# C products of a state-space stage on GpSimd, fed by DMA and summed in PSUM

## The reference

```
u = silu(conv1d(u) + conv1d_b);  x_dbl = u @ x_proj_w.T
dt, Bm, Cm = x_dbl[..., :8], x_dbl[..., 8:16], x_dbl[..., 16:]
delta = softplus(dt @ dt_proj_w.T + dt_proj_b);  A = -exp(A_log)
# for every position t:
h = exp(delta_t * A) * h + (delta_t * u_t) * B_t      # (D, N)
y_t = sum over n of h[:, n] * C_t[n]
# then
y = (y + u * D_param) * silu(z);  out = y @ out_proj_w.T
```

## Time and profile before

| | us |
|---|---|
| median of 3 runs (450.05 to 451.16) | 450.65 |
| the profiled execution | 448.37 |
| its span | 446.7 |
| busy TensorE / VectorE / ScalarE / GpSimd | 366.8 / 330.4 / 302.2 / 177.2 |
| first scan starts / last scan starts | 153.13 / 302.46 |

### The profile page before, as it was taken

The page is one execution under the profiler, slowest core; times in us unless marked ns, Lnnn a source line. Parts: engine busy times, 40 slices in busy tenths (PEclk is TensorE's granted clock), DMA queues, the critical chain, the costliest instruction groups (busy, mean ns, idle before and its releaser), DMA issues. The chain is left out here.

```text
span 446.7 us, 10932 instructions
## 1 busy us (share of the span) xinstructions
PE 366.8 (82%) x4013; PEld 240.8 (54%) x4013; DVE 330.4 (74%) x603; ACT 302.2 (68%) x619; POOL 177.2 (40%) x149
## 2 busy tenths in 40 slices
PE   5699999999995959986785746567797989999996
PEld 5567777777653421432242212123484649888885
DVE  1779887787832896799987999996666876655554
ACT  2389899999855897588759925518985454454543
POOL 7134223313103339839955996766171220000000
PEclk9679999999998995689987966868999999999999
DMA  6110000005040320050000000000030000111111
GB/s 157 6 20 6 1 0 1 0 0 119 9 106 20 72 54 1 2 124 0 0 0 1 1 0 0 0 0 1 1 74 1 1 2 15 19 24 21 21 21 26
DMA packets 24447, 10.34 MB, mean 23 GB/s; under 512 B 20976, under 2 KB 22768, under 8 KB 24416
## 3 DMA queue, kind: packets, MB, share of 16 engines
q1 hardware_dynamic: 23624, 9.87, 10.8%
q10 hardware_dynamic: 792, 0.07, 0.2%
HBM read 2.00 MB, written 1.61 MB: 8 GB/s over the span
## 5 line engine op out<-in xcount | busy, mean ns | idle before, releaser
L1357 PE MATMUL pair<-BCf,sel 96*128 96x392 bf16 x128 | 38.2, 392 | 32.8 <-DVE Hs L1947 28.8
L493 POOL TENSOR_TENSOR YA<-YA,hC 128x784 f32<-128x784 f32 x27 | 51.0, 1887 | 31.1 <-DVE hC L1963 30.1
L1947 DVE TENSOR_TENSOR_SCAN Hs<-dA,pair 128x784 f32<-128x784 f32 x32 | 57.1, 1785 | 1.2 <-ACT dA L833 0.3
L462 POOL TENSOR_TENSOR Km<-Ks,mask 128x784 f32<-128x784 f32 x16 | 24.1, 1507 | 69.2 <-ACT Ks L713 69.2
L1357 PEld LDWEIGHTS pair<-BCf,sel 96*128 96x128 bf16 x128 | 10.2, 104 | 71.2 <-issue 68.5
L1836 DVE TENSOR_REDUCE mx<-pair 128x8 f32<-128x392 f32 x64 | 33.0, 556 | 19.2 <-PE pair L1145 19.2
L1940 DVE TENSOR_TENSOR pair<-DU,pair 128x784 f32<-128x784 f32 x32 | 31.1, 973 | 11.1 <-PE pair L1357 10.7
L1183 PE MATMUL pair<-ident,Pr 128*128 128x128 f32 x256 | 38.5, 284 | 0.5 <-ACT Pr L700 0.5
L1656 PE MATMUL pair<-hst,BD 128*128 128x112 f32 x224 | 37.0, 295 | 2.2 <-DVE Rt L2242 0.5
L1183 PEld LDWEIGHTS pair<-ident,Pr 128*128 128x128 f32 x256 | 29.0, 144 | 11.5 <-issue 9.6
L1656 PEld LDWEIGHTS pair<-hst,BD 128*128 128x128 f32 x224 | 29.2, 190 | 9.5 <-DVE hst L2236 5.4
(11 more groups left out here) (259 smaller groups left out, 885.6 us busy)
## 6 DMA issues: line engine op xcount, KB each, us to landing
SX<-XP SPq DMA_DIRECT2D x48, 112.2 KB
XT<-in_x SPq DMA_DIRECT2D x4, 392.0 KB, 6.3
out<-Os SPq DMA_DIRECT2D x28, 56.0 KB, 1.7
AD<-Aa SPq DMA_DIRECT2D x4, 196.0 KB
NB<-in_L_conv_x_proj_w SPq DMA_DIRECT2D x4, 3.0 KB
DW<-in_L_conv_dw SPq DMA_DIRECT2D x4, 1.1 KB
W<-in_L_conv_w_qkv ACTq DMA_DIRECT2D x1, 48.0 KB
vec<-in_L_conv_b_qkv ACTq DMA_DIRECT2D x3, 0.5 KB
```

The source lines that it names most:

```text
L493: eng.tensor_tensor(y, y, hC[:, n % NHC, :], ALU.add).then_inc(g_ya, 1)
L1357: ins = eng.matmul(SPREAD[s][:, columns(h)], sel[:, n, :], upper(BCf[:, c % 2, s, columns(h)]), start=True, stop=True)
L1947: eng.tensor_tensor_scan(Hs[:, n % 2, :], dA[:, n % NA, :], SPREAD[0], 0.0, ALU.mult, ALU.add).then_inc(v_s, 1)
```

## The change

C no longer goes through TensorE's spread. B and C are projected in one product of 128 columns: rows 0 to 95 hold three copies of B for the bf16 parts, rows 96 to 127 the 8 rows of C of the four groups. A DMA on SP's queue hands row n of C to all channels, in one of four buffers Cs. GpSimd multiplies the states by it (`times_c`), with four buffers of states and three of products, and TensorE adds the products into PSUM (STATES, pair 1) with 32 x 32 pieces of the identity (`total`). VectorE loses its C products; its B product comes in halves of 392 columns, each of which waits for its half of the spread alone. The softplus drops the correction's factor exp(-log(u)) = 1/u, takes the log from another table set, and writes the relu straight into DL; for image 0 VectorE does relu and the copy of the projection. The orders of all engines are written anew.

```diff
-        PAIR = dict(B=0, C=1, conv=2, u=2, delta=2, xC=2, xB=3, wout=3, out=3, var=3, z=3, x2=3)
+        PAIR = dict(B=0, conv=2, u=2, delta=2, xB=2, wout=3, out=3, var=3, z=3, x2=3)
...
+            def c_rows(c, *states):
+                for n in states:
+                    i = DS * c + n
+                    if n == 0:
+                        eng.wait_ge(c_["xB"], c + 1)
+                    if i >= NCS:
+                        eng.wait_ge(v_c, i - NCS + 1)
+                    eng.dma_start(Cs[i % NCS][:, :], bcast(BCf[3 * C + n:P:DS, c % 2, :], 1, C)).then_inc(s_cs[i % NCS], 16)
+            shifted_copies(0)
+            shifted_copies(1)
+            c_rows(0, 0, 1, 2, 3)
+            shifted_copies(2)
+            c_rows(0, 4, 5, 6, 7)
+            c_rows(1, 0, 1)
+            shifted_copies(3, (0,))
+            c_rows(1, 2)
+            shifted_copies(3, (1,))
+            c_rows(1, 3)
+            shifted_copies(3, (2,))
+            c_rows(1, 4, 5, 6, 7)
+            c_rows(2, *range(DS))
+            c_rows(3, *range(DS))
...
+            def times_c(c, *states):                       # GpSimd
+                for n in states:
+                    i = DS * c + n
+                    eng.wait_ge(s_cs[i % NCS], 16 * (i // NCS + 1))
+                    eng.wait_ge(v_s, i + 1)
+                    if i >= NHC:
+                        eng.wait_ge(y_s, i - NHC + 1)
+                    eng.tensor_tensor(hC[:, i % NHC, :], Hs[:, i % NHS, :], Cs[i % NCS][:, :], ALU.mult).then_inc(v_c, 1)
...
                 elif i == 1:                               # GpSimd, pool_ssm
+                    times_c(1, 0, 1)
                     remainder(2)
+                    times_c(1, 2)
+                    split(2)
+                    times_c(1, 3, 4)
                     plus_log(2)
                     delta(2)
+                    times_c(1, 5)
                     scaled(0)
+                    times_c(1, 6, 7)
...
                 elif i == 1:                               # ScalarE, act_ssm
                     silu_u(2, 0)
                     silu_u(2, 1)
                     silu_z(1)
+                    exponents()                            # a table load
                     decays(1, 4)
                     sp_abs(2, 0)
                     sp_abs(2, 1)
                     sp_e(2)
                     sp_u(2)
                     sp_u1(2)
                     decays(1, 5)
                     sp_relu(2)
                     copy_bc(2)
                     out_m(0)
                     decays(1, 6)
                     var_ln(0)
                     var_exp(0)
                     decays(1, 7)
+                    log(2)                                 # a table load and sp_l
                     silu_conv(3, 0)
                     silu_conv(3, 1)
                     silu_x2(2)
+                    exponents()
                     decays(2, 0, 1, 2, 3)
...
+            def add_up(src, h, first=False, last=False):   # TensorE
+                for g in range(G):
+                    rows = slice(C * g, C * g + C)
+                    ins = eng.matmul(STATES[rows, h, :], ident[rows, rows], src[rows, columns(h)], start=first, stop=last)
+                return ins
...
+                elif i == 1:                               # TensorE, pe_ssm
+                    spread(1, 1)
+                    total(0, 6, 7)
+                    inner(2, 1)
+                    spread(1, 2)
+                    total(1, 0)
+                    gate(1)
+                    delta(2, 0)
+                    delta(2, 1)
+                    spread(1, 3)
+                    total(1, 1)
+                    x_b(2)
+                    spread(1, 4)
+                    total(1, 2)
+                    out(0)
+                    spread(1, 5)
+                    total(1, 3)
+                    conv(3, 0)
+                    var(0)
+                    spread(1, 6)
+                    total(1, 4)
+                    conv(3, 1)
+                    spread(1, 7)
+                    total(1, 5)
+                    x2(2)
+                    spread(2, 0)
+                    total(1, 6)
+                    inner(3, 0)
...
             def times_b(c, n):                             # VectorE
                 eng.wait_ge(v_du, c + 1)
+                for h in range(2):
+                    eng.wait_ge(p_["B"], 2 * (DS * c + n) + h + 1)
+                    eng.tensor_tensor(SPREAD[:, columns(h)], DU[:, c % 2, columns(h)], SPREAD[:, columns(h)], ALU.mult).then_inc(v_b, 1)
             def scan(c, n):
+                i = DS * c + n
+                eng.wait_ge(v_b, 2 * i + 2)
+                eng.wait_ge(a_da, i + 1)
+                if i >= NHS:
+                    eng.wait_ge(v_c, i - NHS + 1)
+                eng.tensor_tensor_scan(Hs[:, i % NHS, :], dA[:, n % NA, :], SPREAD, 0.0, ALU.mult, ALU.add).then_inc(v_s, 1)
...
+            def first_rows():                              # VectorE, image 0, inside the last attention step
+                eng.wait_ge(p_["xB"], 1)
+                eng.tensor_copy(halves(BCf[:, 0, :]), result("xB", 0)).then_inc(c_["xB"], 1)
+                remainder(0)
```

More of the change, by code:

```diff
@@ L560, in pool_ssm @@
                 if i == 0:
-                    add(0, 1)
-                    split(1, 0, "xB")
-                    remainder(1)
-                    add(0, 2)
+                    times_c(0, 0, 1, 2, 3, 4)
+                    split(1)
                     plus_log(1)
-                    add(0, 3)
                     delta(1)
-                    split(1, 1, "xC")
-                    add(0, 4)
-                    add(0, 5)
-                    add(0, 6)
-                    add(0, 7)
+                    times_c(0, 5, 6, 7)
@@ L954, in act_ssm @@
                     decays(2, 7)
-                    decays(3, 0, 1, 2, 3)
+                    log(3)
                     silu_z(3)
                     silu_x2(3)
+                    exponents()
+                    decays(3, 0, 1, 2, 3)
                 else:
@@ L997, in _ @@
             turned(1)
-            eng.activation(early_ln[:, :], epsc[:, :], ACT.Ln)
+            eng.preload_act_table_set(LN_EXP)
             eng.wait_ge(g_nt0, J - 1)
@@ L1417, in pe_ssm @@
-                    inner(2, 0, (0,))
-                    bc("C", 6)
-                    inner(2, 0, (1, 2))
-                    spread(1, "B", 0)
+                    spread(0, 5)
+                    total(0, 2)
+                    x2(1)
+                    spread(0, 6)
+                    total(0, 3)
+                    conv(2, 0)
+                    spread(0, 7)
+                    total(0, 4)
+                    conv(2, 1)
+                    spread(1, 0)
+                    total(0, 5)
@@ L1461, in pe_ssm @@
+                    total(1, 6)
+                    inner(3, 0)
+                elif i == 2:
+                    spread(2, 1)
+                    total(1, 7)
+                    inner(3, 1)
+                    spread(2, 2)
+                    total(2, 0)
+                    gate(2)
                     delta(3, 0)
                     delta(3, 1)
+                    spread(2, 3)
+                    total(2, 1)
+                    wout(0)
                     x_b(3)
-                    bc("B", 1)
@@ L1490, in pe_ssm @@
+                    total(2, 5)
+                    x2(3)
+                    spread(3, 0)
+                    total(2, 6)
+                else:
+                    spread(3, 1)
+                    total(2, 7)
                     wout(1)
-                    bc("C", 1)
+                    spread(3, 2)
+                    total(3, 0)
                     out(2)
-                    bc("B", 3)
-                    bc("C", 2)
-                    bc("B", 4)
+                    spread(3, 3)
+                    total(3, 1)
+                    spread(3, 4)
+                    total(3, 2)
@@ L1496, in pe_ssm @@
                     var(2)
-                    bc("C", 3)
-                    bc("B", 5)
-                    bc("C", 4)
-                    bc("B", 6)
-                    bc("C", 5)
+                    spread(3, 5)
+                    total(3, 3)
+                    eng.wait_ge(a_ud, 1)
+                    for h in range(2):
+                        add_up(S1[:, 0, 0:T], h)
+                    spread(3, 6)
+                    total(3, 4)
                     wout(2)
-                    bc("B", 7)
@@ L1504, in pe_ssm @@
-                    bc("C", 6)
+                    spread(3, 7)
+                    total(3, 5)
                     eng.wait_ge(c_["var"], J - 1)
                     spare(5, 4)
-                    bc("C", 7)
+                    total(3, 6)
                     spare(4, 4)
+                    for h in range(2):
+                        eng.wait_ge(v_c7, h + 1)
+                        add_up(hC[:, (DS * J - 1) % NHC, :], h, False, True).then_inc(y_s, 1)
             eng.wait_ge(s1z, 1)
```

473 lines of the change are left out of this document (171 added, 302 removed).

## The result

The changed kernel takes 460.12 us in the median of four runs (456.09 to 460.63), the kernel before took 450.35 on the same chip (447.56 to 451.16): a ratio of 1.0204, with an interval of 1.0157 to 1.0251. It is 2.0% slower, and the whole interval lies above 1. The forecast was 458, within 452 to 470. The profiled execution has a span of 458.8 us, before 446.7; at 460.63 us it is the slowest of the four.

A forecast was written before the change was run, and what follows sets the result against it. VectorE was taken to bound the kernel before, busy 32 to 37 of each image's 35 to 41 us. Terms -8.2 -7.3 +13.4 +7.0 -5.5 -0.5 +8.2 = +7.1 on 448.37: 455.5 profiled, 458 median, range 452 to 470.

The forecast's parts named there:

- Start: Start of the state stage: first scan at 144.9 instead of 153.13, -8.2 us.
- A state: One state on VectorE: B product, scan and bare round trip of 0.6, 3.5 us; TensorE's sum 1.4 warm.
- Image 0: First image, scan to scan: 33.4 us, was 40.7, so -7.3, with TensorE hardly pausing ahead of the convolutions.
- Images 1 and 2: Middle images: two waits each make them 48.4 and 44.8 us, +13.4 and +7.0, before cold costs.
- First wait: Images 1 and 2: x_B and the spread behind it wait for ScalarE's relu, 4.9 us lost on VectorE's line.
- Second wait: Before the next image's first scan: log, GpSimd's product 5, sum, x2 and silu delay it 6.3 us in image 1.
- Cold products: TensorE at low clock after idling in images 1 and 2: 4.1 us an image, +8.2 in all.
- Image 3: Last image, no softplus, VectorE sets the pace: 30.3 us to the last scan, was 35.8, so -5.5.
- Tail: End of the kernel: a table load without the small logarithm behind it, -0.5 us.
- C by DMA: C rows on SP's queue: four engines, 4.4 to 7.2 us a DMA; taken as hidden at the fast end.
- the DMA rival: C DMAs bound the stage: four engines at the shift copies' rate, 7.2 us each, 528 us; chance 0.17.
- Waits given back: Rival, faster: waits and cold stretches vanish; half of 30 us gone gives 443, all gone 428; chance 0.33.

The follow-up runs named there:

- an eighth of each row: Against the changed kernel, 28 of the 32 C DMAs move only 98 of 784 columns of every row: 458.40 us, ratio 1.0250.
- the fillers: Against the changed kernel, TensorE does 30 or 60 small unread products in its waits ahead of x_B and total(1,5), total(2,5): 455.86 us, ratio 1.0173.
- the B product in one: Against the changed kernel, VectorE's B product is one instruction of 784 columns that waits for both spread halves: 456.47 us, ratio 1.0174.
- row 4 moved: On top of GpSimd's order, the DMA of C row 4 of image 0 stands ahead of image 2's shift copies: 434.76 us, ratio 0.9685.
- GpSimd's order: On top of the other two edits, GpSimd makes products 0 to 3 before remainder and split in images 1 and 2: 436.12 us, ratio 0.9726.
- the other two edits: Against the changed kernel, relu right behind the absolutes; softplus log earlier, GpSimd's product 5 earlier, silu of x2 later: 440.40 us, ratio 0.9865.

## Why the prediction was right, and where its terms were off

The sign, the place and the mechanism were as forecast: two waits in each of images 1 and 2 that the written orders make. The sum, +7.1 us for the profiled execution, came out as +12.1 us of span, and as +9.8 from median to median. Last scan to last scan it is +13.1 (315.55 for 302.46). By the prediction's terms:

*Start,* -8.2 forecast, -7.2 measured (145.91 for 153.13). The softplus remainder took 2.08 us and the addition of the log 1.93, each for the 1.6 of the row. But among executions of one and the same code up to there the first scan moved by 1.8 us (144.06 to 145.91, so -9.1 to -7.2), and the forecast lies within that.

*A state.* 3.5 us forecast, 3.45 measured; bare round trip 0.6 forecast, 0.59; sum 1.4 forecast, 1.52 warm, so the four column groups do overlap. GpSimd's product was 1.94 for the 1.85 to 1.89 of the additions.

*Image 0,* -7.3 forecast, -1.9 measured: the step that failed. The prediction said that TensorE hardly pauses ahead of the convolutions there, and took all of image 0 at the full clock. The convolutions did run warm (2.18 a half). But behind them TensorE paused 2.02 us for the first scan, ahead of spread(0,1), and another 0.80 for a silu, and ran cold from 148 to 155, through inner:

```profile
147.84 0.51 PE L1359 MATMUL pair<-BCf,sel 96*128 96x392 bf16 x2 [2.02 <-DVE Hs L1962]
149.15 4.29 PE L1310 MATMUL pair<-S,BD 128*128 128x392 f32 x6 [0.80 <-ACT S L782]
153.23 0.86 PE L1359 MATMUL pair<-BCf,sel 96*128 96x392 bf16 x2
```

Half of inner took 4.29 us where it takes 2.24 warm; delta(1) and the relu stand behind it, and x_B began 20.2 us after the first scan where the walk had 17.4. That is 2.8 of the 5.4 us missed. The other 2.6 is the second cold stretch, behind the wait for the relu, which the walk did not count for this image and which other executions escape: three of them (an eighth of each row, the fillers, the B product in one) have image 0 at 35.7 to 36.1, near -5. The C row that GpSimd waits for here (6.22 us, until 169.29) did not matter in the changed kernel: with it landed early, in the run with an eighth of each row, the image is no shorter than in other executions without the cold x_B (35.7 for 36.0 and 36.1). Nor is it shown to matter once the relu is early: with row 4 moved image 0 took 32.4 in one run and 35.3 in another, for 35.2 without.

*Images 1 and 2,* +17.5 and +11.1 forecast with their cold parts, +17.5 and +10.7 measured. The sizes hold; the division inside them holds less well, and that they agree to 0.4 us is in part luck. "First wait, 4.9 us lost": VectorE's wait was 7.54 and 5.89, but moving the relu, alone, won nothing. The prediction had named the reason in one sentence (GpSimd is held too, remainder before product 2) and had not seen that this chain alone is as long. So it was not one semaphore there but two that end together, the relu for x_B and minus one for the remainder. GpSimd's order, moved on top of the other two edits, won 4.3 us (6.2 by the ratios); it was not tried without the early relu, so whether the relu has to move at all is not shown. "Second wait, 6.3 us": moving it won 10.1 and 9.7. That is its 6.3 and 6.2 with the cold sum (1.3) and the cold x2 (1.0) behind it, and about 1.4 more that the runs do not divide; in that run both are warm behind the last states of image 1 (1.52 and 1.59). Cold products cost an image 4.1 by the forecast; in TensorE's rows of image 1 the excess is 1.4 for x_B, 0.3 for its spread, 1.0 and 1.3 for the sums and 1.1 for x2, together 5.1. The forecast put all of it on VectorE's line. The runs show 2.6 of the stretch at x_B there in image 0, but 1.4 of 2.65 in image 2 (with the fillers); for the stretch behind the second wait they show no price of its own.

*Image 3,* -5.5 forecast, -6.1 measured. *Tail,* -0.5 forecast, -1.0 (span +12.1 for the last scan's +13.1).

*C by DMA.* Four engines, as the packet count says, and hidden: moving an eighth left images 1 and 2 as they were. One took 3.9 us where the walk took 4.4 as its fast end, so the DMA rival, with up to 7.2, fell. By the Trainium skill (DMA: Bandwidth & Descriptors, section Why a DMA increments its semaphore by 16 and not by 1) the outermost dimensions that are not of size 1 give 4 engines here and 16 for DMAs of one row onto 32. Both agree with the packets, 132 and 48. The Trainium skill (SBUF — State Buffer, section Door 1: The DMA port swizzle) puts partitions 32 apart on one port. The halving that the prediction read out of it was not seen: the four carried 25.8 GB/s each, more than the 22.9 of the earlier trace rows.

*Waits given back,* the rival on the other side, did not happen: its condition, fewer than 22 of the 30 us of waits, was not met in the orders as written. It named the size well, though. With most of the waits taken out by order alone the kernel takes 431.5 us, and that rival had 428 for all of them gone and 443 for half.

## What to carry to other kernels

Taking work off the busiest engine pays only what the orders of the others let through: walk each queue past the new waits before trusting a sum of busy times. Where two chains end at the same point, shortening one of them can win nothing, as the relu did here, so look for the second before moving the first. Work whose result is used late (a silu, a variance) belongs behind work that starts the next recurrence: together with a product moved ahead of the softplus that was worth 10 us an image here. When the waits are gone, look for the resource that was hidden behind them, here the DMA queue. And where the clock falls in some executions and not in others, compare a part of the kernel over several runs before its gain is put down to an edit.

## What the hardware showed that was not expected

- More engines moved less: four engines, for one DMA of four rows onto 128, carried 103 GB/s together; 16 engines, for DMAs of one row onto 32 and with the same bytes in all, 71 GB/s at a share of 0.88, and a C row took 5.7 us for 3.9. Why is not shown.
- A DMA issue can hold the engine that makes it. Ten issues on ScalarE's queue, beside C rows on SP's, took 15.88 us, and the activation behind them waited 16.70; alone at the start of the program most issues took 0.5 to 0.6 us on SP's queue. It is not ScalarE's queue as such: with row 4 moved, four shift copies between C rows took 6.10 and 6.28 us to issue on SP's, where no other work stands behind them but DMAs.
- A wait of nearly the same length (2.81 and 2.94 us) left TensorE at the upper level of its clock in one execution (granted 1.00 from 168 to 172) and at the lower in another (0.50), which was worth 2.6 us in one image: 0.6% of a run, as much as some of the edits above won.
- The same VectorE instruction, the normalisation XP of 784 columns, took 0.67 us at 147.61 in the changed kernel and 3.60 in the run with GpSimd's order, where two GpSimd additions (172.48 and 174.45) overlapped it. No experiment moved it, so that GpSimd caused it is likely and not shown.
